# Slot compares in a mixture-of-experts kernel: sixteen per unit with a scalar each, or two with both operands broadcast

## The reference

```python
k = int(EXPERT_CAP * t / NUM_EXPERTS)            # 2 * 2048 / 8 = 512
probs = jnp.transpose(softmax(x @ gate_w), (0, 2, 1))
g, m = jax.lax.top_k(probs, k)                   # 512 rows for each batch and expert
xin = jax.vmap(lambda xb, mb: xb[mb])(x, m)
h = gelu(xin @ w1) @ w2
out = zeros.at[m].add(g[..., None] * h)          # then the gated residual
```

## Time and profile before

| | |
|---|---|
| median of 3 runs | 1247.05 us (1243.36 to 1248.24) |
| profiled execution | 1243.3 us, of which the span from first to last instruction is 1241.5 us |
| mean granted TensorE clock | 0.931 of full speed |
| busy: TensorE / VectorE / ScalarE / POOL | 1085.9 / 794.5 / 673.3 / 438.8 us |
| the compares of line 1500 | 512 instructions, 86.9 us of VectorE's busy time |
| memory traffic | 118.05 MB, 95 GB/s on average |

### The profile page before, as it was taken

How to read it: one execution, slowest core, us unless ns; L and a number is a source line. 1 busy time by engine, 2 the same in 40 slices (tenths; PEclk the granted TensorE clock), 3 DMA queues, 4 the chain that set the end, 5 groups by cost and what they waited for, 6 DMA issues and landing times.

```text
span 1241.5 us, 19213 instructions
## 1 busy us (share of the span) xinstructions
PE 1085.9 (87%) x7110; PEld 965.3 (78%) x7110; DVE 794.5 (64%) x2197; ACT 673.3 (54%) x1025; POOL 438.8 (35%) x349
## 2 busy tenths in 40 slices
PE   6588899878863599999999999999999999989980
PEld 5477788767653499888988988998998898878970
DVE  3678999988967678776435645644454564457452
ACT  2347777665520554565466556556645655665541
POOL 1012221120100343454345345435434534556443
PEclk8789999988975699999999999999999999999985
DMA  6004634222110343343223434433423424337565
GB/s 208 0 18 153 205 135 170 86 77 64 51 54 32 107 110 80 74 86 75 43 44 54 110 71 87 118 63 55 91 37 73 89 44 120 53 102 238 162 181 183
DMA packets 84158, 118.05 MB, mean 95 GB/s; under 512 B 16865, under 2 KB 69729, under 8 KB 83041
## 3 DMA queue, kind: packets, MB, share of 16 engines
q1 hardware_dynamic: 57168, 81.80, 19.5%
q0 software_dynamic: 24576, 34.10, 16.7%
q10 hardware_dynamic: 2320, 0.93, 0.3%
HBM read 66.21 MB, written 50.59 MB: 94 GB/s over the span
## 4 chain that ended last, share of the span: by engine, by line
PE 59%; DVE 3%; issue 1%; ACT 1%; DMA 1%; POOL 1%; DVEq 0%; SPq 0%; POOLq 0%; ACTq 0%
PE psum L1660 29%; PE psum L1683 27%; PE psum L1631 2%; DVE hidT L1539 1%; PE psum L1640 1%; DVE idx_cur L1511 1%; DMA rows_in<-z_rows,idx_cur 0%; DVE place L1500 0%; POOL ffn_rows L1378 0%; ACT hf L1446 0%; DMA w_raw<-ffn_rows 0%; POOL rows_in L1366 0%; DMA ffn_rows<-rows_y,idx_cur 0%; POOL w_raw L1281 0%; ACT acc L1432 0%
## 5 line engine op out<-in xcount | busy, mean ns | idle before, releaser
L1660 PE MATMUL psum<-w,hidT 128*128 128x256 f32 x3072 | 379.9, 285 | 11.6 <-DVE hidT L1539 11.6
L1660 PEld LDWEIGHTS psum<-w,hidT 128*128 128x128 f32 x3072 | 372.8, 191 | 12.5 <-DVE hidT L1539 12.4
L1683 PE MATMUL psum<-xT,w 128*128 128x512 f32 x1536 | 373.2, 398 | 3.9 <-DVE xT L1526 3.9
L1539 DVE TENSOR_TENSOR hidT<-hf,hidT 128x512 fp32r<-128x512 f32 x256 | 182.2, 721 | 268.5 <-ACT hidT L1450 268.4
L1683 PEld LDWEIGHTS psum<-xT,w 128*128 128x128 f32 x1536 | 285.3, 189 | 65.6 <-DVE xT L1526 4.3
L1378 POOL DMA_INDIRECT ffn_rows<-rows_y,idx_cur x128 | 201.6, 1575 | 373.9 <-ACT rows_y L1423 344.7
L1423 ACT ACTIVATE rows_y<-psum,g_cur 128x256 f32<-128x256 f32 x128 | 53.7, 471 | 260.3 <-PE psum L1660 250.3
L1446 ACT ACTIVATE hf<-psum 128x512 f32<-128x512 f32 x256 | 152.9, 597 | 65.2 <-PE psum L1683 43.1
L1366 POOL DMA_INDIRECT rows_in<-z_rows,idx_cur x128 | 149.1, 1165 | 92.8 <-DVE idx_cur L1511 48.7
L1450 ACT ACTIVATE hidT<-hf 128x512 fp32r<-128x512 f32 x256 | 161.9, 632 | 8.2
L553 POOL TENSOR_SCALAR ve<-mv 128x4 f32<-128x4 f32 x32 | 17.5, 546 | 314.1 <-DVE mv L698 314.1
(11 more groups left out here) (189 smaller groups left out, 1253.6 us busy)
## 6 DMA issues: line engine op xcount, KB each, us to landing
w_raw<-in_L_ffn_w SPq DMA_DIRECT2D x20, 1024.0 KB, 5.5
x_buf<-in_L_attn_x SPq DMA_DIRECT2D x16, 512.0 KB, 5.1
ffn_rows<-scratch SPq DMA_DIRECT2D x8, 1024.0 KB, 7.2
x_rows<-x SPq DMA_DIRECT2D x16, 512.0 KB, 2.8
z_rows<-z SPq DMA_DIRECT2D x16, 512.0 KB, 3.1
w_raw<-ffn_rows SPq DMA_DIRECT2D x16, 512.0 KB, 6.0
scratch<-x_rows SPq DMA_DIRECT2D x12, 512.0 KB, 5.6
out_x<-scratch SPq DMA_DIRECT2D x12, 512.0 KB, 4.3
```

The source lines that it names most:

```text
L1539: dve.tensor_tensor(hidT[1][:, m, :], hf[m % HF][:], hidT[0][:, m, :].bitcast(F32), ALU.subtract).then_inc(f_hl, 1)
L1660: ins = pe.matmul(Y_tok[:, t, :], hidT[qs][:, k, t * P:(t + 1) * P], w2_s[n % 2][qm][:, k, :], start=(x_ == 0), stop=(x_ == len(terms) - 1))
L1683: ins = pe.matmul(H_bank[m % 4], w1_s[n % 2][qs][:, k, m * P:(m + 1) * P], xT[qm][:, k, :], start=(x_ == 0), stop=(x_ == len(terms) - 1))
```

## The change

Two edits. `slot_u` becomes bf16, so that the copy of line 1487 also casts (the numbers are 0 to 127). The eight `tensor_scalar` compares of a half, each with one tile's slot number as its per-partition scalar, become one `tensor_tensor` compare of 128 x 8 x 128: `row_id` is repeated for each tile, and each slot number is repeated along the 128 columns. The result is the same tensor, written in the same order by halves, with the same semaphore.

```diff
-        slot_u = [sbf(f"slot_u{n}", [P, ST, 1]) for n in range(2)]
+        slot_u = [sbf(f"slot_u{n}", [P, ST, 1], BF16) for n in range(2)]
...
                 def places_of(u, half):
 
                     n = u % 2
-                    for t in range(half * ST // 2, (half + 1) * ST // 2):
-                        ins = dve.tensor_scalar(place[n][:, t, :], row_id[:], slot_u[n][:, t, 0:1], None, ALU.is_equal)
-                    ins.then_inc(f_pl, 1)
+                    at = slice(half * ST // 2, (half + 1) * ST // 2)
+                    dve.tensor_tensor(place[n][:, at, :], row_id[:].unsqueeze(1).to_broadcast([P, ST // 2, P]),
+                                      slot_u[n][:, at, :].to_broadcast([P, ST // 2, P]), ALU.is_equal).then_inc(f_pl, 1)
```

## The result

| | before | after |
|---|---|---|
| median of 5 runs | 1247.05 us (1243.36 to 1248.24) | 1235.16 us (1233.68 to 1235.76) |
| ratio after / before | | 0.9907, 95% interval 0.989 to 0.9924 |
| profiled execution, span | 1243.3, 1241.5 us | 1235.76, 1233.6 us |
| mean granted TensorE clock | 0.931 | 0.926 |
| VectorE busy, instructions | 794.5 us, 2197 | 784.0 us, 1749 |

The kernel is 11.9 us faster by the medians, 0.93% by the ratio. The prediction was no change (1247.0, range 1242.5 to 1250.5), with 0.03 for faster: it was wrong. The medians and ratios of this document leave out one execution, of e3, that took 1816.58 us at a granted clock of 0.552.

What follows compares the result with a forecast made beforehand. The prediction took TensorE's end-to-end layer 1 and 2 matmuls as the bound. Its terms, +0.3 for unit 0's gathers and -0.35 for unit 6, summed to -0.05 us: 1247.0 us against a median of 1247.05, range 1242.5 to 1250.5.

Steps and rivals of the forecast that it cites:

- What bounds the kernel: Steady stretch, 600 to 1100 us: TensorE's layer 1 and 2 matmuls end to end, 23.92 us a unit, never waiting for VectorE.
- What one new compare costs, 1.22 us: VectorE: 1024 elements at the rate of line 1491's bf16 product; bounds 0.69 us and some 2.4 us.
- the packed and the slow case: Rivals on compare speed: packed, 0.61 us per half, 1244.4 us, chance 0.08; slow, 2.4 us per half, 1259 us, chance 0.04.
- The pair against the sixteen, -0.33 us: VectorE, each unit: two new compares take 2.36 us against 2.69 for sixteen; 10.6 us in all, almost all in gaps.
- Gathers held: Unit 0's third and fourth POOL gathers, held by unit 1's compares: fourth ends 0.6 us late, landing taken as +0.3.
- The lower bound, that it follows the weights' transfer: Landing of unit 0's fourth gather: -0.33 us if it follows the weights, which are also issued earlier.
- Unit 6, -0.35: Compares for unit 8's list: halves shorter by 0.19 + 0.16 us, taken from TensorE's 1.09 us wait.
- Units 1 to 5, and units 7 on, 0: No effect: VectorE has 0.8 us in hand in units 1 to 5; later compares lie in a 6.65 us gap.
- a steady unit that is not 23.92 us: Steady stretch: one of the signs listed as showing the prediction wrong; unit length was to stay 23.92 us.
- the 0.02 given to unseen gains: Whole kernel: 0.08 chance for what was not seen, half no change, a quarter each way, so a quarter for faster.
- The sum, -0.05 us for the compares: Whole kernel: +0.3 for unit 0's gathers and -0.35 for unit 6; bounds -0.7 and +0.3.
- the prediction's lower bound of -0.7: Whole kernel: -0.33 at unit 0 and -0.35 at unit 6; as rival "gathers not held", 1246.4 us, chance 0.2.

Runs made afterwards that it cites:

- e3: New compares with xT at its old address and 64 more unused bytes ahead of hidT, so only hidT shifts against its weights; 1230.13 us, ratio 0.9897.
- e2: Changed kernel with an unused 64-byte tensor behind the slot numbers, so new compares in the old layout; 1248.11 us, ratio 1.0008.
- e14: Kernel before with 768 extra layer 2 matmuls at its end, run on with other engines idle; 171 matmuls in 20 us, 118.7 ns each.
- e15: Changed kernel with the same 768 extra layer 2 matmuls at its end; 179 matmuls in 20 us, 113.3 ns each, other engines idle.
- e1: Kernel before with its second slot tensor allocated last, so old compares in the changed kernel's layout; 1234.25 us, ratio 0.9903.
- e13: Kernel before with only the experts' weights and small tensors behind them 64 bytes further on, xT and hidT unmoved; 1227.54 us, ratio 0.9852.
- e9: e3 with 64 unused bytes also ahead of x_buf, shifting first-half operands hT_z and hT against their weights; 1241.86 us, ratio 0.9958.
- e10: Changed kernel with 128 unused bytes ahead of hidT; 1238.32 us, ratio 0.9936.
- e12: The sixteen old compares in e10's layout; 1237.80 us, ratio 0.9928.
- e16: Changed kernel with 64 unused bytes ahead of the experts' weights, giving e13's layout with new compares; 1227.97 us, ratio 0.9864.

## Why the prediction was wrong, step by step

- **What bounds the kernel: right.** TensorE's matmuls end to end. This is why a few ns in each of them counted in full.
- **What one new compare costs, 1.22 us: right** (1222 ns, 1217 to 1227). The row with the same operand pattern gave it, and the packed and the slow case both fell. That agrees with the Trainium skill, "Vector Engine (DVE) Microarchitecture Reference", Performance modes, which has one repeated 2-byte element run at one per cycle. The case that this section leaves open, both operands one repeated element, is not this one: here the first operand is a repeated row.
- **The pair against the sixteen, -0.33 us: right** (2.36 against 2.69). VectorE's busy time fell by 10.5 us, for 10.6 worked out; nearly all of it went into gaps like the one of 6.93 us.
- **Gathers held: right in size, wrong in effect.** The third lasted 1.93 us (1.9 foreseen), and the fourth began when the second compare was over, 10.75 us after the first compare's start, as worked out. But the landing did not follow the gather: from first compare to turning it took 0.47 us less, not 0.3 more; in e2, 15.29 us against 15.67, 0.38 less. Over all 18 profiles it is 15.20 to 15.63 us with the new compares and 15.67 to 15.84 with the old. The lower bound, that it follows the weights' transfer, was the right one: from the first compare's start the weights landed at 15.29 us and the last gather at 15.79 in e14 (old compares), at 14.63 and 15.36 in e15 (new), so both came earlier though that gather started later.
- **Unit 6, -0.35: right.** TensorE's wait went from 1.09 to 0.89 us in the changed kernel and to 0.74 in e2, where 0.75 was foreseen. From its turning to the next, unit 6 took 26.28 us before and 25.95 in e2, 0.33 less.
- **Units 1 to 5, and units 7 on, 0: here it failed.** For the compares it was true: in e2 units 1 to 5 take 24.58 to 24.59 us and the later ones 23.92, as before. What failed is the step "The copy of slot numbers now casts 16 elements (I take 0; ...)": it priced the edit of `slot_u` as an instruction and not as an allocation, and so took the length of TensorE's matmuls as fixed. By the prediction's own sign, a steady unit that is not 23.92 us, it is refuted. Halving the tensor moved `xT` and `hidT` by 64 bytes, and 0.41 us a unit came from that, more than from all that the prediction had in its sum. No rival covered it, and the 0.02 given to unseen gains was too little for a change that resizes a tensor in the middle of a layout.
- **The sum, -0.05 us for the compares: e2 measured 1.0008 (0.9995 to 1.0022)**, so it stands within what can be measured. Term by term, e2's profile gives -0.38 and -0.33, the prediction's lower bound of -0.7; the +0.3 for the gathers had the wrong sign.

How the 11.9 us come about: in the profiled executions the stretch of the units gives 8.0 and the end 1.5 us, of which 2.1 - 0.5 us is taken off at the start, by chance and by the first list. The rest, some 4 us, is mostly that the profiled execution of before lies 3.7 us below its median. The stretch would have given more, but for the unit behind the residual gates: from the turning of unit 30 to that of unit 31 it took 27.3 us before and takes 30.2 after. The chain of the changed kernel just ahead of it:

```profile
1129.83 4.43 DVE hidT L1539
...
1136.74 3.85 DVE hidT L1539 x3
```

A low-half subtraction now meets POOL's gates there and is held, as the index addition of rows 13 was. e1 has 30.2 us too, e2 27.4 and e13 27.2, so it does not come with the compares. Nor does it come with the layout alone: e14, whose compares and addresses are those of before, took 31.2 us there, 3.9 more than the profile of before. Such a meeting in its other executions would also account for the 3.7 us between the profiled execution of before and its median. All this was seen, not tested by itself.

## What to carry to other kernels

An edit that changes the size of an on-chip tensor also moves every tensor behind it. Before crediting an instruction, compare the addresses of both programs and run the pair that separates them: the new instructions in the old layout, and the old ones in the new. In a kernel bound by fp32 matmuls of 256 to 512 columns it is worth trying 64 unused bytes between the tensors of a product's two operands; measure each layout, since the same distance modulo 128 gave 1227.5 us here in one and 1238.3 in another, and nothing in the first half of the block.

## What the runs showed of the hardware

- TensorE's matmul interval depended on where its two operands start relative to one another: 118.6 ns at distance 0 modulo 128 bytes and 113.3 at 64 for 256 columns, 232.6 and 229.2 for 512 columns, at full granted clock, and for 256 columns also with all other engines idle (171 against 179 matmuls in 20 us). At 32 bytes it was slowest (119.9 and 234.2, one execution each). In the first half of the block the same move brought next to nothing in e9: 119 to 118 ns for 256 columns, 232 to 233 and 234 for 512.
- At distance 64 layer 2 has two steady patterns, 113.4 and 117.8 ns, held for a whole unit. Which one comes is open: it differed between e3 and e9, whose experts' tensors have the same addresses, between e10 and e12, which differ in the compares, and between the changed kernel and e16, where the operands are equally many bytes apart.
- An indirect gather that POOL started beside a VectorE compare with two SBUF inputs lasted 1.93 us and ended 0.82 us after that compare (413.30 against 412.48 us); the compare that followed did not hold it again. Beside compares with one tensor input and a scalar it lasted 0.96 us, alone 0.95.
